# Attention's output and the network's input transposed by SP's DMA queue, V's bias added at V's eviction: a fused attention and feed-forward layer on eight cores

## What is computed

```
Q, K, V = x @ Wq + bq, x @ Wk + bk, x @ Wv + bv          # 16 heads of 64, per sequence of 4096 rows, 1024 wide
w       = softmax(causal(Q K^T / 8))
x       = layernorm(x + (w V) @ Wo + bo)
x       = layernorm(x + (silu(x wg^T / 127) * (x wu^T / 127)) @ (wd / 127)^T)     # hidden 3072
```

## Time and profile before

| | us |
|---|---|
| median of 3 runs | 1165.81 (1165.63 to 1166.45) |
| the profiled execution | 1166.87 |
| its span on the slowest core, core 2 (role 0) | 1165.2 |
| the other even cores' spans | 1162.1 to 1163.9 |
| the odd cores' spans | 1160.5 to 1162.8 |
| PE busy on core 2 | 1118.3 |
| ACT busy, DVE busy on core 2 | 602.1, 390.9 |

### The profile page before, as it was taken

The page is one execution under the profiler, slowest core; times in us unless marked ns, Lnnn a source line. Parts: engine busy times, 40 slices in busy tenths (PEclk is TensorE's granted clock), DMA queues, the critical chain, the costliest instruction groups (busy, mean ns, idle before and its releaser), DMA issues.

```text
span 1165.2 us, 28546 instructions; the slowest of 8 cores (1160.5 to 1165.2 us)
## 1 busy us (share of the span) xinstructions
PE 1118.3 (96%) x11460; PEld 676.3 (58%) x11568; DVE 390.9 (34%) x833; ACT 602.1 (52%) x723; POOL 87.9 (8%) x156
## 2 busy tenths in 40 slices
PE   3899999999999999999999999999999999999997
PEld 1676677767676677765555566666444444444443
DVE  0333323333333433335667522222333212121333
ACT  0588889999999899898855411112000111111000
POOL 3000000000000000013010211111000111110000
PEclk9999999999999999999999999999999999999999
DMA  9902100021001103069655764334111345441011
GB/s 128 155 3 38 21 2 3 2 39 21 2 3 21 20 3 74 33 153 244 138 129 109 147 107 73 63 65 73 37 55 55 74 75 82 78 73 19 37 45 66
DMA packets 32200, 74.61 MB, mean 64 GB/s; under 512 B 3648, under 2 KB 9792, under 8 KB 31168
## 3 DMA queue, kind: packets, MB, share of 16 engines
q0 software_dynamic: 26448, 54.80, 28.4%
q1 hardware_dynamic: 5616, 17.91, 4.1%
HBM read 109.65 MB, written 8.91 MB: 102 GB/s over the span
## 4 chain that ended last, share of the span: by engine, by line
PE 93%; issue 2%; DMA 2%; DVE 2%; ACT 1%; POOL 0%; POOLq 0%; DVEq 0%; ACTq 0%
PE ps_s L850 15%; PE ps_s L856 15%; PE bank_o L826 11%; PE ps_s L794 11%; PE ps_s L767 10%; PE ps_u L697 7%; PE ps_u L716 7%; PE ps_u L708 5%; PE ps_u L767 5%; PE ps_u L732 4%; DMA x<-x 2%; PE ps_s L732 1%; PE bank_o L746 1%; ACT PT L897 1%; PE ps_s L753 0%
## 5 line engine op out<-in xcount | busy, mean ns | idle before, releaser
L897 ACT ACTIVATE PT<-ps_s 128x1024 bf16<-128x1024 f32 x510 | 490.2, 1024 | 56.0 <-PE ps_s L794 48.9
L911 ACT ACTIVATE gs<-ps_s 128x384 bf16<-128x384 f32 (+1 forms) x120 | 63.9, 533 | 260.3 <-PE ps_s L850 260.1
L850 PE MATMUL ps_s<-x1T,wgb 128*128 128x384 bf16 (+1 forms) x953 | 195.5, 347 | 0.4
L856 PE MATMUL ps_s<-x1T,wub 128*128 128x384 bf16 (+1 forms) x952 | 195.3, 347 | 0.4
L826 PEld LDWEIGHTS bank_o<-V,PT 128*128 128x128 bf16 x4080 | 155.8, 97 | 46.9 <-issue 23.1
L826 PE MATMUL bank_o<-V,PT 128*128 128x65 bf16 x4080 | 176.4, 193 | 2.4 <-DVE PT L1006 2.0
L794 PE MATMUL ps_s<-Q2T,K2T 64*128 64x256 bf16 (+1 forms) x2736 | 158.4, 244 | 4.0 <-ACT PT L897 1.5
L1028 DVE TENSOR_TENSOR hT<-ps_s,gs 128x384 bf16<-128x384 f32 (+1 forms) x120 | 73.3, 611 | 264.3 <-PE ps_s L856 252.7
L850 PEld LDWEIGHTS ps_s<-x1T,wgb 128*128 128x128 bf16 x960 | 93.8, 98 | 83.2
L856 PEld LDWEIGHTS ps_s<-x1T,wub 128*128 128x128 bf16 x960 | 93.9, 98 | 82.6
L767 PE MATMUL ps_s<-wd_sb,hT 128*128 128x512 bf16 x541 | 120.2, 379 | 0.6
(11 more groups left out here) (57 smaller groups left out, 599.2 us busy)
## 6 DMA issues: line engine op xcount, KB each, us to landing
wgb<-wg POOLq DMA_DIRECT2D x48, 256.0 KB, 4.1
wub<-wu POOLq DMA_DIRECT2D x48, 256.0 KB, 5.1
xq_sb<-bo SPq DMA_DIRECT2D x17, 512.0 KB, 5.2
xq_sb<-xq POOLq DMA_DIRECT2D x17, 512.0 KB, 11.1
y<-y SPq DMA_DIRECT2D x17, 512.0 KB, 2.7
wd_sb<-wd POOLq DMA_DIRECT2D x6, 1024.0 KB, 14.2
x<-x POOLq DMA_DIRECT2D x4, 1024.0 KB, 28.2
wk_sb<-wk POOLq DMA_DIRECT2D x8, 256.0 KB, 4.6
```

Source lines behind the costliest of these rows:

```text
L850: inst = pe.matmul(ps_s[w % 2][:, 0, 0:n], wgb[:, i % 4, ec, :], x1T[:, ec, q:q + n], start=(ec == 0), stop=(ec == NEC - 1))
L856: inst = pe.matmul(ps_s[w % 2][:, 1, 0:n], wub[:, i % 4, ec, :], x1T[:, ec, q:q + n], start=(ec == 0), stop=(ec == NEC - 1))
L897: act.activation(PT[:, no % NSLOT], ps_s[no % 3][:], AF.Exp, scale=SCALE).then_inc(sem_exp, 1)
L911: act.activation(gs[:, no % 2, 0:n], ps_s[no % 2][:, 0, 0:n], AF.Silu, scale=1.0 / 127.0).then_inc(sem_silu, 1)
```

## The change

1. Attention's output: PE's 'O' items, `ps_t`, `rows_in` on DVE and the identity go. SP issues a transposing DMA for each 128 rows, from `o_nat` to `o_allT` (after.py L584), two per block of 256.
2. The network's input: PE's 'T' units and DVE's copies go. SP issues eight transposing DMAs a set, from `x1` to `x1T` (after.py L592), with one semaphore per group of sets.
3. V's bias is added by DVE where V leaves PSUM (a `tensor_add` in place of a copy); `bv` is now loaded as 128 x 1024 f32 (512 KB) at the start, where it lies in the place of `xq_sb`'s slot for set 4. So SP's loads of `bo` are in another order: slots 2 and 3 at once at the start, 0, 1 and 4 after the last V unit.
4. SP's program follows DVE's list item by item and waits in that order. `normalised(b)` waits for the transposes of block b - 2, since `o_nat` has two buffers. 'W' units may start one block earlier (`block_end[... qt // 2] + 6` for `block_end[... qt // 2 + 1] + 5`, in steps). POOL's `load_gu(4)` moves ahead of a wait that now counts the last transposes of attention's output.

The core of the diff:

```
         for qt in range(NROWS):
-
-            first = self.block_end[nb * (NPAIR - 1) + qt // 2 + 1] // (4 * STEP) + 5
+            first = self.block_end[nb * (NPAIR - 1) + qt // 2] // (4 * STEP) + 6
             rows += [(first, self.steps, ('W', qt, 0)), (first, self.steps, ('W', qt, 1))]
-            if qt:
-                rows.append((first, self.steps, ('T', qt - 1)))
         self._spread(out, rows, range(begin, self.steps))
...
         w = 0
         for qt in range(NROWS, role.nset):
             if qt > NROWS:
-                unit('T', qt - 2)
                 unit('W', qt, 0)
                 self.dve.append(('N', qt - 1))
             unit('W', qt, 1)
-            if qt == NROWS + 1:
-                self.pe.append(('O', nb - 1))
-                self.dve.append(('B', nb - 1))
             self._waves(w)
             self.act.append(('R', qt))
             w += 1
-        unit('T', role.nset - 2)
         self.dve.append(('N', role.nset - 1))
         self._waves(w)
-        unit('T', role.nset - 1)
         w += 1
...
         def sync_program(sp):
-            for qt in range(role.nset):
-                if qt < 2:
-
-                    sp.wait_ge(sem_unit, plan.all_done('V', 3))
-                elif qt == 5:
-
-                    sp.wait_ge(sem_unit, plan.all_done('K', 7))
-                    sp.wait_ge(sem_unit, plan.all_done('Q', 7))
-                elif qt >= 12:
-                    sp.wait_ge(sem_ev, plan.done('W', xq_slot(qt), 1))
+            def rows_in(b):
+
+                sp.wait_ge(sem_o, b + 1)
+                p, q, n = block_rows(b)
+                for i in range(n // 128):
+                    sp.dma_start(o_allT[:, p, q + 128 * i:q + 128 * i + 128], o_nat[:, b % 2, i, :],
+                                 transpose=True).then_inc(sem_ot[b % 2], 16)
+
+            def rows_on(qt):
+
+                sp.wait_ge(sem_n, qt + 1)
+                g = next(i for i, sets in enumerate(plan.groups) if qt in sets)
+                for ec in range(NEC):
+                    sp.dma_start(x1T[:, ec, qt * 128:(qt + 1) * 128], x1[:, qt, ec * 128:(ec + 1) * 128],
+                                 transpose=True).then_inc(sem_xt[g], 16)
+
+            def load_bo(qt):
                 sp.dma_start(xq_sb[xq_slot(qt)][:], d['bo']).then_inc(sem_bo[xq_slot(qt)], 16)
+
+            load_bo(2)
+            load_bo(3)
+
+            for what, no in plan.dve:
+                if what == 'D':
+                    rows_in(no)
+                elif what == 'N' and no < role.nset:
+                    rows_on(no)
+                elif what == 'E' and no + 1 == plan.all_done('V', 3):
+
+                    sp.wait_ge(sem_ev, no + 1)
+                    for qt in (0, 1, 4):
+                        load_bo(qt)
+                elif what == 'E' and no + 1 == max(plan.all_done('K', 7), plan.all_done('Q', 7)):
+
+                    sp.wait_ge(sem_ev, no + 1)
+                    for qt in range(5, 12):
+                        load_bo(qt)
+                elif what == 'E' and plan.units[no] in [('W', xq_slot(qt), 1) for qt in range(12, role.nset)]:
+
+                    sp.wait_ge(sem_ev, no + 1)
+                    load_bo(plan.units[no][1] + 8)
...
                 load_qk(p)
 
-            pool.wait_ge(sem_pv, plan.block_end[nblock * 6 - 1] // 4 + 1)
+            pool.wait_ge(sem_pv, plan.pv_count[plan.block_end[nblock * 6 - 1]])
             pool.dma_start(wo_sb[:], d['wo']).then_inc(sem_wo, 16)
-            for qt in range(5):
+            for qt in (2, 3, 0, 1, 4):
                 add_rows(qt)
...
-            pool.wait_ge(sem_pv, ntile)
+            pool.wait_ge(sem_pv, len(plan.pv_count))
             for c in range(3):
                 load_wd(c)
-
-            pool.wait_ge(sem_tr, NPAIR * nblock)
             load_gu(4)
+
+            for i in range(2):
+                pool.wait_ge(sem_ot[i], ot_count(len(plan.block_end) - 1 - (len(plan.block_end) - 1 - i) % 2))
...
-                if nblock * 7 + qt // 2 + 1 > seen_ot:
-                    seen_ot = nblock * 7 + qt // 2 + 1
-                    pe.wait_ge(sem_ot, seen_ot)
+                b = nblock * 7 + qt // 2
+                if b >= seen_ot:
+
+                    seen_ot = b + 1
+                    if qt < 2:
+                        pe.wait_ge(sem_ot[(b - 1) % 2], ot_count(b - 1))
+                    pe.wait_ge(sem_ot[b % 2], ot_count(b))
-            def block_out(b):
-
-                nonlocal seen_o
-                if b == 0:
-                    pe.wait_ge(sem_const, 16 * len(consts))
-                if b + 1 > seen_o:
-                    seen_o = b + 1
-                    pe.wait_ge(sem_o, b + 1)
-                for i in range(block_rows(b)[2] // 128):
-                    inst = pe.transpose(ps_t[:, i * 128:(i + 1) * 128], o_nat[:, b % 2, i, :], ident[:])
-                inst.then_inc(sem_tr, 1)
-
-            def transposed(qt, ps):
-                pe.wait_ge(sem_n, qt + 1)
-                out = ps.bitcast(BF16).rearrange("p (e k) -> p e k", k=128)
-                for ec in range(NEC):
-                    inst = pe.transpose(out[:, ec, :], x1[:, qt, ec * 128:(ec + 1) * 128], ident[:])
...
-                if hc == 0 and plan.done('T', (q + n - 1) // 128) > seen_ev:
-                    seen_ev = plan.done('T', (q + n - 1) // 128)
-                    pe.wait_ge(sem_ev, seen_ev)
+                if hc == 0:
+
+                    g = next(k for k, sets in enumerate(plan.groups) if (q + n - 1) // 128 in sets)
+                    pe.wait_ge(sem_xt[g], 16 * NEC * len(plan.groups[g]))
...
-                    dve.tensor_copy(V2[:, a % 2, c[0]:c[-1] + 1, :, 0:64],
-                                    ps[:, 0:256 * len(c)].rearrange("p (c h f) -> p c h f", h=4, f=64)
-                                    ).then_inc(sem_ev, 1)
-
-            def rows_in(b):
-
-                dve.wait_ge(sem_tr, b + 1)
-                p, q, n = block_rows(b)
-
-                dve.tensor_scalar(o_allT[:, p, q:q + n], ps_t[:, 0:n], bv_sb[:, p:p + 1], None,
-                                  ALU.add).then_inc(sem_ot, 1)
+                    if unit == ('V', 0, 0):
+                        dve.wait_ge(sem_bv, 16)
+                    dve.tensor_add(V2[:, a % 2, c[0]:c[-1] + 1, :, 0:64],
+                                   ps[:, 0:256 * len(c)].rearrange("p (c h f) -> p c h f", h=4, f=64),
+                                   bv_sb[:, a].rearrange("p (h f) -> p h f", f=64).unsqueeze(1)
+                                   .broadcast_to([128, len(c), 4, 64])).then_inc(sem_ev, 1)
...
 
-                if b:
-
-                    dve.wait_ge(sem_tr, b)
-                else:
-                    dve.wait_ge(sem_block, 1)
+                dve.wait_ge(sem_pv, plan.pv_count[plan.block_end[b]])
                 n = block_rows(b)[2] // 128
                 dve.reciprocal(rec[:, b % 2, 0:n], ps_o[:, 0:n, :, 64]).then_inc(sem_rec, 1)
-                if b:
-                    rows_in(b - 1)
+                if b >= 2:
+
+                    dve.wait_ge(sem_ot[b % 2], ot_count(b - 2))
                 dve.wait_ge(sem_rec, b + 1)
                 dve.tensor_mul(o_nat[:, b % 2, 0:n].rearrange("p q (h f) -> p q h f", f=64),
                                ps_o[:, 0:n, :, 0:64],
...
-                    elif unit[0] == 'T':
-                        qt = unit[1]
-                        dve.tensor_copy(x1T[:, :, qt * 128:(qt + 1) * 128],
-                                        ps.bitcast(BF16).rearrange("p (e k) -> p e k", k=128)
-                                        ).then_inc(sem_ev, 1)
...
                 sp.dma_start(dst[:], d[name]).then_inc(sem_const, 16)
+            sp.dma_start(bv_sb[:], d['bv']).then_inc(sem_bv, 16)
             role = sp.alloc_register('role_sp')
```

More of the change, by code:

```diff
@@ L108, in __init__ @@
         self.tiles = [range(h, min(h + 4, n)) for h in range(0, n, 4)]
+        ends = sorted({t[-1] for t in self.tiles} | set(self.block_end))
+        self.pv_count = {h: i + 1 for i, h in enumerate(ends)}
         self.steps = -(-len(self.tiles) // STEP)
@@ L148, in __init__ @@
             self.pass_end.append(len(self.waves) - 1)
+            for q in parts:
+                have = sum(map(len, self.groups))
+                self.groups.append(range(have, -(-(q + part) // 128)))
             q0 = q1
@@ L278, in _products @@
             return None
-        block = self.block_end.index(h)
-        if block:
-            self.pe.append(('O', block - 1))
-        return block
+        return self.block_end.index(h)
     def _shares(self):
@@ L487, in build @@
     sem_pv = sem('sem_pv')
-    sem_block = sem('sem_block')
+    sem_bv = sem('sem_bv')
     sem_rec = sem('sem_rec')
     sem_o = sem('sem_o')
-    sem_tr = sem('sem_tr')
-    sem_ot = sem('sem_ot')
+    sem_ot = [sem(f'sem_ot{i}') for i in range(2)]
     sem_bn = sem('sem_bn')
@@ L497, in build @@
     sem_n = sem('sem_n')
+    sem_xt = [sem(f'sem_xt{i}') for i in range(5)]
     sem_g = sem('sem_g')
```

(14 more changed lines are left out.)

28 lines of the change are left out of this document (10 added, 18 removed).

## The result

The changed kernel takes **1223.9 us** (median of 4 runs) against 1165.81 before: 1.0492 times as long, 95% interval 1.0470 to 1.0514. The forecast was 1153.5 us, the range 1147 to 1190; both missed, and the first rival (SP's queue is the bound), which had 0.30, describes best what happened.

A forecast was written before the change was run, and what follows sets the result against it. The prediction took PE as the bound. Core 3, slowest after the change, came to 1162.8 - 14.0 saved + 4 at the start = 1152.8 us; adjusted for span and run median, the forecast was 1153.5 us, range 1147 to 1190.

The forecast's parts named there:

- the first rival: SP's queue: over 1.0 us per transposing DMA makes it the bound; 1190 us at 1.5, 1226 at 2.0; chance 0.30.
- What bounds it now: Whole kernel: PE's time counts almost one for one, except in the first 28 us, where loads count.
- What leaves PE: Transposes in attention (0.14 us a block) and network input, plus waits: 18.0 us off core 2, 14.0 off core 3.
- The 'T' units' term: PE's transposes of the network's input: 7.6 us saved on an even core, 6.7 on an odd one.
- Is ACT close behind?: Attention: ACT's load of 36.36 in 39.2 us stays under PE's, binding only in single steps, so attention's gain stands.
- that rival: Attention held by ACT's steps gives nothing back, only the network's 'T' units do: 1162.2 us; chance 0.05.
- DVE's add at V's eviction: V's eviction on DVE: the add takes 692 ns where the copy took 694, so it costs nothing.
- The division's wait: nothing: DVE's division waits for block b - 2's transposes: 4.1 us between divisions, landing 2.0, margin about 1.5, no cost.
- The start: 4 us: Kernel's start: early loads of bv and bo delay PE's x by 4 us on every core, bounds 0 to 5.2.
- The price of a transposing DMA, 0.45 to 0.9 us: SP's queue time per transpose, t: free below about 1.0 us, above it 7.3 us per 0.1 us.
- Other edits: nothing: Earlier 'W' units, SP's late loads of bo and POOL's held-back network weights: all priced at nothing.
- Odd cores last: End of the run: core 3, an odd core, is slowest at 1152.8 us against core 2's 1151.2.

The follow-up runs named there:

- e15: The changed kernel with four buffers for the divided output, one transposing DMA per set of the network's input, and the start's loads as before; 1183.36 us.
- e16: Attention's output by transposing DMA in the first seven pairs only, four buffers, all other transposes on PE, the start's loads as before; 1165.62 us, ratio 0.9989.
- e13: The changed kernel with all transposes back on PE and the start's loads as before, V's bias still added at V's eviction; 1166.62 us, ratio 1.0005.
- e2: The changed kernel with the network's input transposed by PE again, attention's output still by SP's DMAs; 1187.06 us, ratio 1.0181.
- e12: Only attention's output transposed by DMA, as against the changed kernel, with four buffers for the divided output in place of two; 1170.09 us, ratio 1.0054.
- e1: The changed kernel with both kinds of transposes back on PE, keeping V's bias add and the early loads of bv and bo; 1171.47 us, ratio 1.0049.
- e9: Only attention's output on SP's DMAs, the network's input on PE, and those DMAs plain copies without transposing; 1181.48 us, one run.
- e8: The changed kernel with one transposing DMA of 128x1024 per set of the network's input in place of eight of 128x128; 1201.42 us, ratio 1.0281.
- e7: The changed kernel with plain copies in place of transposing DMAs for the network's input; attention's output still transposed by DMA; 1194.47 us, one run.

## Why the prediction was wrong, point by point

**What bounds it now** held: PE's time counts, e15's core 3 shows it.

**What leaves PE** was right in kind but oversized: on core 3 9.5 us came off where 14.0 were forecast, on core 6 9.7 where the sum for an even core had 18.0. The term that failed is 0.14 us a block in attention, which measured 0.055 to 0.08. The 'T' units' term fits: from e16 to e15, which moves all of them and the last of attention's pairs off PE, core 3 gains 6.6 us, and 6.7 were forecast for the 'T' units. The prediction took the distance between starts in the timeline. I read the difference as steps that ACT holds, since its row has 36 of 40 us; no run tried that alone, so it stays open.

**Is ACT close behind?** Attention's gain did not vanish, so that rival is out, but at 0.055 to 0.08 us a block it came to about half of what the sum had.

**DVE's add at V's eviction** costs nothing: right (693 ns, e13).

**The division's wait: nothing** was wrong, one of the two steps that failed. The margin of 4.1 us was set against a landing of 2.0, read from a load at 2.45 us, when the DMA engines were busy for 0.28 of their time. The landings that held DVE came beside POOL's 2 MB load of wo and beside the full engines before the network (14.9 and 25.8 us on core 6 of e2), not at the pairs' starts where the prediction looked. PE on core 6 pays 16.9 us for it in the change, and e12 shows the cause by taking it away with two more buffers.

**The start: 4 us** was right: core 2's waits for x grew by 2.8 us (16.2 to 19.0) and core 6's by 5.1 (15.4 to 20.5), the second projection of K stands 3.3 and 5.1 us later on them, and 4.9 us lie between e1 and e13.

**The price of a transposing DMA, 0.45 to 0.9 us** was the step that failed most. It is 1.22 to 1.24 us, over the threshold of 1.0 that the prediction had worked out rightly. The plain DMA of the same shape does take 0.466 (e9), so the bounds 0.43 and 2.0 were sound; wrong was to choose near the lower end because the row was "of the same shape and the same issuer", where no row was of the same operation. At t = 1.24 the prediction's slope gives 1153.5 + 0.24 x 73 = 1171 us. The rest of the way to 1224 is that t was 1.96 for the first 16 and so 1.49 over the whole stretch on core 6 (0.49 x 73 = 36 us in place of 18), that the last transfer of the group landed 16.2 us after its issue (the chain of core 6, at 671.55 us) and not 2.0, and that the division's waits, 16.9 us, moved attention itself. Together that is 1153.5 + 36 + 14.2 + 16.9 = 1221 us, an estimate, as no run shows how far the three overlap.

**The other figure for t.** The Trainium skill's page "VectorE: DVE Perf Modes", section "The three transpose paths", gives 1309 ns for a 128x128 transpose by DMA. The spacing of 1.22 to 1.24 us in SP's queue agrees with it within 7%, better than the neighbour row that the sum was made from. The same page's advice, which stands in its section "Rules for kernel authors", is to transpose 128x128 by TensorE where PSUM will do as destination. It fits too: no version with all transposes on DMA beat the kernel before.

**Other edits: nothing** holds for the weights that POOL holds back until the last block's transposes: in e2 and e12, which hold them back too, no core waits for wu. What had no term at all is that the transposes of the network's input delay the weights that POOL loads beside them. Core 6 waits 6.8 us for wu in the change and e8's core 5 23.9 us; e7 has no such wait.

**The account**, core 2 against its span before: +52.5 us. Waits added: 30.3 for x1T, 17.6 for the division, 5.3 for wu, 2.8 for x (19.0 against 16.2), together 56.0. Off goes PE's relief; cores 3 and 6 of e15 put it at 9.5 and 9.7. That leaves 6 us, an estimate from unlike cores, for which the slower clock behind the stalls is the likely cause; no run shows it apart.

**Odd cores last**: wrong. In the profiled execution they end 4 to 9 us before the even ones.

**Range and chances.** The first rival's size at t = 2.0, 1226 us, came out for a t of 1.25; its formula lacked the landing and the second wait. Its probability was too small for what spoke for it: two measured bounds around the threshold and a page's figure beyond it.

## What to carry to other kernels

Price an operation that the trace lacks by its own kind, not by the neighbour of the same shape; if the threshold lies inside the bounds, both sides deserve nearly equal chances. When a transfer takes a compute engine's place, look at the fullest stretch of the DMA row between its issue and its use, and give it buffers for the latest landing there, not the median. A version that uses the transfers only where the engines are idle, and keeps the start of before, got 0.2% here; the whole move cost 4.9%.

## What the runs showed of the hardware

- A transposing DMA of 128x128 bf16 holds SP's queue 1.22 us (median), a plain copy of the same blocks 0.466 (e9); one of 128x1024 holds it 1.30 us when little is under way (e8, core 2), and six held it 89.93 us beside POOL's loads (e8, core 5).
- A transfer of 32 KB that lands in 1.9 to 3.0 us in the median took 20.2 us (plain, e9, core 2) and 31.4 us (transposing, the change, core 6) at worst; the late ones stand beside full DMA engines. That median is for attention's output; for the network's input it was 5.2 us.
- The clock falls after a stall of PE. Windows of core 6 (busy PE, PEld, DVE, ACT, POOL, then PEclk, DMA share, GB/s):

```profile
560.00:580.00 20.00, 13.86 (x193) 8.82 (x198) 7.93 (x16) 9.95 (x12) 0.44 (x1) 0.79 0.99 176
...
660.00:680.00 20.00, 2.94 (x14) 1.15 (x12) 4.16 (x7) 1.89 (x4) 2.47 (x4) 0.69 0.80 167
680.00:700.00 20.00, 11.93 (x58) 6.35 (x60) 4.72 (x8) 6.26 (x8) 2.62 (x5) 0.72 0.80 133
```

After the wait that ends at 688.01 us eight matmuls take 2.72 us, and 1.46 us at 695.67. The granted clock is 0.50, the 1.2 GHz level, from 688 to 690 us and 1.00 again from 693. So a stall costs more than its length. The prediction had no term for it.
